# The context's key, value and output products taken out of the attention turns and put between the tiles of the q, k, v projection

## The chip, the cores and the metric

One core of one Trainium2 chip runs one program. The metric is the device time of one execution in microseconds (us), median of three runs. Engines: TensorE (PE), VectorE (DVE), ScalarE (ACT), GpSimd (POOL) and SyncE (SP), which issues every DMA here.

## The reference

A decoder layer on 16 batches of 128 tokens of width 1024, all in 32-bit floats, with a context of 16 x 128 x 1024:

```python
x = x + attn(layernorm(x))              # qkv = clip(x Wqkv^T, +-8); layer norm of q and k; 32 heads with ALiBi; Wout
x = x + xattn(layernorm(x), ctx, ctx)   # linear attention, below
x = x + ffn(layernorm(x))               # silu(x W1) * (x W3), then W2; weights unpacked from 4 bits

# xattn, per batch; q, k, v are [128, 1024] (128 tokens are the channels, 1024 the length n)
kh = softmax(Wk @ ctx, axis=-1)                    # 512 x 1024
vh = Wv @ ctx
qh = softmax(Wq @ xn, over the 64 of a head) * 64**-0.5
context = kh vh^T per head (8 heads of 64 x 64)
out = Wo @ (context^T qh) + bo ; normalised over the 128 channels, times g
```

What depends on the context alone (kh, vh, their product, and Wo on it: a matrix z of 128 x 512 for each batch) needs nothing of x.

## The kernel before

The program has three phases, one after the other. Each has a written-out instruction order for each engine, with semaphores between them.

**Projection** (`qkv_phase`, L155). x is normalised and transposed once (`LayerNormT`, L41), and split in a high and a low part of type fp32r. The weights come in 6 chunks of 512 columns, each in 8 slices of 128 x 512: SP loads a slice to one of two places in `stage` (L197), ACT writes its high part (L231), DVE the low part (L255). For each chunk, 16 tiles of 128 tokens are computed: `product` (L309) runs 24 matmuls of 512 columns (8 slices of the inner dimension by the three terms high*high, high*low, low*high). DVE clips the tile (L282), SP stores it (L217). A slice is loaded every second tile, before the wait for that tile's clip (L215, L216); ACT splits it in every even tile (L246), DVE in the odd ones (L278), so that the last slice of a chunk is split a tile before it is needed. Four PSUM banks take the tiles in turn.

**Attention** (`attention_phase`, L316). Turn b computes the self-attention of batch b ("own") and, interleaved, the cross attention of batch b-1 ("cross"); turn 0 is own alone, turn 16 cross alone. A turn has 12 steps and a tail. In step t PE does, in this order (L510): transposes of the probabilities of head group t-2 (L519), scores of group t (L527), the cross query product of tile t-2 (L537), the value product of group t-3 (L548), then the context's part: the keys of its tile (L558, t = 0, 2, 4, 6), the transposes of their exponentials (L564, t = 1, 3, 5, 7), the key by context product (L575, t = 3, 5, 8, 9), then the transposes of the query softmax (L584). In the last two steps come the value product (L589) and the output product (L595). These context products are plain 32-bit matmuls; a plain one is recorded as two matmuls. The steps' other engines: DVE sums the query's exponentials (L736), adds the bias (L481), takes the maximum (L487), the query's maximum and difference (L749, L752) and a reciprocal (L765); ACT the exponentials (L656, L662) and copies (L652, L666); POOL two scalings (L697, L708). The tail of the turn on PE: output of the cross attention (L604), first half of the Wout projection, transposes of the next q and k (L421), the norm (L626), second half of the projection, transposes of the next context (L438), and the broadcast of the norm (L643). After it DVE scales (L821) and starts the next turn's first scores.

**Feed-forward** (`feed_forward_phase`, L915): not touched.

## Time and profile before

| | |
|---|---|
| three runs | 3303.15, 3303.19, 3303.97 us; median 3303.19 |
| span of the profiled execution, first to last instruction | 3299.9 us (the page gives no other time of it) |
| busy: PE, PE weight load | 3128.8, 2393.9 us |
| busy: DVE, ACT, POOL | 1773.3, 1045.8, 507.1 us |
| mean granted clock of TensorE | 0.977 |

The page gives busy shares of each engine over the span; a row of the trace gives the start of an instruction, its length, and what ended its engine's idle time before it. Matmuls are pipelined: the record of one overlaps the next, so the time that one takes from PE is the distance between two starts, not the length of a record.

### The profile page before, as it was taken

To read this page: it belongs to the slowest core of one execution; us is meant where nothing else is said; L and a number is where in the kernel's file an instruction comes from. 1 tells how busy PE (TensorE), PEld (TensorE's weight loads), DVE (VectorE), ACT (ScalarE), POOL (GpSimd) and SP (SyncE) were. 2 spreads that over 40 slices of the span, in tenths; PEclk is the share of its full clock that TensorE was granted. 3 is DMA by queue.
4 is the path that set the end of the run, shared out by engine and by line. 5 is a ranking of instruction groups with operands and counts; after the bars stand their busy time and mean duration, and the time that the engine had idled before them with its cause. 6 is when DMAs were issued, how large, how long until landed. Compare 5 with 4: busy or idle time off the path is not lost. (4 is left out here: it accounts for less than half of the span.)

```text
span 3299.9 us, 41826 instructions
## 1 busy us (share of the span) xinstructions
PE 3128.8 (95%) x15136; PEld 2393.9 (73%) x15136; DVE 1773.3 (54%) x2927; ACT 1045.8 (32%) x2356; POOL 507.1 (15%) x525
## 2 busy tenths in 40 slices
PE   7999997799999999999996799999999899999998
PEld 6888886566666666666663688888887788888887
DVE  5311112466666666666663655555555655555555
ACT  2100000566665566666651211111111211111111
POOL 2100000233333333333332100000000100000000
PEclk9999999899999999999996899999999999999999
DMA  4222223111111111111110432222122521231222
GB/s 144 93 73 75 73 70 116 41 39 38 43 46 51 38 38 39 50 38 51 38 33 31 129 82 55 76 65 75 54 82 76 153 64 54 81 81 54 62 74 78
DMA packets 83350, 218.73 MB, mean 66 GB/s; under 512 B 11984, under 2 KB 18256, under 8 KB 81232
## 3 DMA queue, kind: packets, MB, share of 16 engines
q1 hardware_dynamic: 83280, 217.78, 21.8%
q8 instruction: 46, 0.75, 0.1%
q14 instruction: 24, 0.20, 0.0%
HBM read 175.79 MB, written 41.94 MB: 66 GB/s over the span
## 5 line engine op out<-in xcount | busy, mean ns | idle before, releaser
L312 PE MATMUL ff_ps<-h_xT_hi,w_hi 128*128 128x512 f32 x1376 | 538.2, 391 | 13.2 <-DVE h_xT_lo L96 13.2
L312 PE MATMUL ff_ps<-h_xT_lo,w_hi 128*128 128x512 f32 x1376 | 537.1, 390 | 0.0
L312 PE MATMUL ff_ps<-h_xT_hi,w_lo 128*128 128x512 f32 x1376 | 537.0, 390 | 0.0
L1042 ACT ACTIVATE w_hi<-words 128x1024 fp32r<-128x1024 f32 x134 | 142.5, 1063 | 697.3 <-DVE words L1087 697.3
L1127 DVE TENSOR_TENSOR acc<-ff_po,acc 128x512 f32<-128x512 f32 x352 | 243.0, 692 | 210.6 <-PE ff_po L312 209.9
L312 PE MATMUL qkv_acc<-w_hi,xT_hi 128*128 128x512 f32 x768 | 300.9, 392 | 9.2 <-DVE w_lo L255 9.2
L312 PEld LDWEIGHTS ff_ps<-h_xT_hi,w_hi 128*128 128x128 f32 x1376 | 259.5, 189 | 68.3 <-issue 8.8
L312 PE MATMUL qkv_acc<-w_hi,xT_lo 128*128 128x512 f32 x768 | 299.4, 390 | 0.0
L312 PE MATMUL qkv_acc<-w_lo,xT_hi 128*128 128x512 f32 x768 | 299.3, 390 | 0.0
L312 PEld LDWEIGHTS ff_ps<-h_xT_hi,w_lo 128*128 128x128 f32 x1376 | 259.4, 189 | 54.1
L312 PEld LDWEIGHTS ff_ps<-h_xT_lo,w_hi 128*128 128x128 f32 x1376 | 259.6, 189 | 53.8
L312 PE MATMUL ff_po<-w_hi,h_hi 128*128 128x512 f32 x704 | 276.3, 393 | 10.1 <-DVE h_lo L1119 10.1
L282 DVE TENSOR_SCALAR qkv_out<-qkv_acc 128x512 f32<-128x512 f32 x96 | 66.4, 692 | 395.1 <-PE qkv_acc L312 395.1
L312 PE MATMUL ff_po<-w_lo,h_hi 128*128 128x512 f32 x704 | 275.8, 392 | 0.0
L312 PE MATMUL ff_po<-w_hi,h_lo 128*128 128x512 f32 x704 | 275.6, 391 | 0.0
L1115 DVE TENSOR_TENSOR gate<-gate,ff_ps 128x512 f32<-128x512 f32 (+1 forms) x88 | 60.3, 686 | 345.4 <-PE ff_ps L312 344.7
L656 ACT ACTIVATE scores<-scores,neg_max 128x128 f32<-128x128 f32 x512 | 199.2, 390 | 120.0 <-DVE neg_max L487 120.0
L231 ACT ACTIVATE w_hi<-w_stage 128x512 fp32r<-128x512 f32 x56 | 35.4, 632 | 452.8 <-DMA w_stage<-in_w_attn 452.8
L697 POOL TENSOR_TENSOR scores<-scores,row_rec 128x512 f32<-128x512 f32 x128 | 133.2, 1041 | 293.3 <-DVE row_rec L765 293.3
L312 PEld LDWEIGHTS qkv_acc<-w_hi,xT_hi 128*128 128x128 f32 x768 | 144.6, 188 | 39.1 <-DVE w_lo L255 9.6
L1087 DVE TENSOR_TENSOR words<-words,sc 128x1024 f32<-128x1024 int32 x134 | 164.2, 1226 | 4.6
L312 PEld LDWEIGHTS qkv_acc<-w_hi,xT_lo 128*128 128x128 f32 x768 | 144.4, 188 | 30.2
(156 smaller groups left out, 5305.9 us busy)
## 6 DMA issues: line engine op xcount, KB each, us to landing
words<-in_w SPq DMA_DIRECT2D x90, 512.0 KB, 3.5
qkv<-qkv_out SPq DMA_DIRECT2D x96, 256.0 KB, 2.0
words<-in_w SPq DMA_DIRECT2D x176, 128.0 KB, 4.0
sc<-in_s SPq DMA_DIRECT2D x88, 256.0 KB, 4.3
qk_in<-qkv SPq DMA_DIRECT2D x16, 1024.0 KB, 4.9
w_stage<-in_w_attn SPq DMA_DIRECT2D x56, 256.0 KB, 3.0
qkv_rows<-in_x SPq DMA_DIRECT2D x16, 512.0 KB, 3.8
ctx_in<-in_context SPq DMA_DIRECT2D x16, 512.0 KB, 3.7
```

The lines of the kernel that those rows point to most:

```text
L231: nc.scalar.activation(dst[:, r, :], stage[:, r % 2, :], ACT.Copy).then_inc(w_hi_done, 1)
L282: nc.vector.tensor_scalar(res[:, :], acc[:, t % BANKS, :], CLIP, -CLIP, ALU.min, ALU.max).then_inc(clipped, 1)
L312: last = nc.tensor.matmul(out, left, right, start=n == 0, stop=n == len(pairs) - 1)
L656: last = nc.scalar.activation(sc[:, t % SR, j, :], sc[:, t % SR, j, :], ACT.Exp, bias=neg_max[:, t, j:j + 1], accum_out=row_sum[:, t, j:j ...
L697: nc.gpsimd.tensor_tensor(sc[:, n % SR, :, :], sc[:, n % SR, :, :], row_rec[:, n, :].unsqueeze(2).to_broadcast([P, HG, P]), ALU.mult).then ...
L1042: nc.scalar.activation(dst, src, ACT.Copy).then_inc(s["split_hi"], 1)
L1087: nc.vector.tensor_tensor(dst, src, scale, ALU.mult).then_inc(s["scaled"], 1)
L1115: nc.vector.tensor_tensor(gate[sl][0:units, :], gate[sl][0:units, :], b, ALU.mult).then_inc(s["product"], 1)
L1127: nc.vector.tensor_tensor(cols, po[:, o % 4, :], cols, ALU.add).then_inc(s["added"], 1)
```

## The change

The context's part leaves the turns and goes into the first phase, now `projection_phase`. There the tokens are taken in two halves of 8 tiles, each with all 6 chunks: 12 rounds of 8 tiles, and every weight slice is loaded and split twice. The order is written out for all 96 tiles, without loops. In rounds 1 to 4 and 7 to 10 the tiles carry the context: batch b takes four tiles, i = 0 to 3. PE does in tile (b, i): the keys of quarter i (`keys`: 2 halves by 3 terms, fp32r), 12 of the tile's 24 matmuls, in tile i = 0 the key by context product of batch b-1 (`key_context`: 24 fp32r matmuls of 512 columns), the 8 transposes of the keys' exponentials (`turn_keys`), the other 12 matmuls; after it, in i = 1 the transposes of the context, in i = 2 the value product and in i = 3 the output product of batch b-1 (both plain 32-bit). z of each batch is stored to memory (`zc`) and loaded by the attention turns. One weight slice of the next round is loaded, split high and split low in every tile. The layer norm of the second half of the tokens is made in round 5. `acc` has two PSUM banks instead of four, `res` two places instead of one. The first round's weights are loaded as four transfers of two slices to places of their own, and the first tile waits for them slice by slice. In attention, the loads of q, k and v of the next batch wait for less (`a_done`, `o_done`), `y` and `y_sq` have their own tiles, and PE's order is otherwise as before.

The core of the diff:

```diff
+    TILES = NB // 2
+    ROUNDS = 2 * QKV_CHUNKS
+    CTX_ROUNDS = (1, 2, 3, 4, 7, 8, 9, 10)
...
+    acc = pb("qkv_acc", [P, 2, N], ph)
+    room_k = pb("room_k", [P, D], ph)
+    room_t = pb("room_t", [P, D], ph)
+    room_u = pb("room_u", [P, D], ph)
...
+    def step(ci, t):
+
+        if ci in CTX_ROUNDS:
+            at = CTX_ROUNDS.index(ci) * TILES + t
+            return at // XT, at % XT
+        if ci == ROUNDS - 1 and t < XT:
+            return NB, t
+        return None, None
...
+            def load(ci, r):
+                sp.wait_ge(s["w_lo_done"], ci * KT + r - 1)
+                chunk = ci % QKV_CHUNKS if ci < ROUNDS else QKV_CHUNKS
+                sp.dma_start(stage[:, r % 2, :], w_attn[chunk, :, r, :]).then_inc(w_in[r % 2], 16)
...
+            for ci in range(ROUNDS):
+                for t in range(TILES):
+                    at = ci * TILES + t
+                    b, i = step(ci, t)
+                    load(ci + 1, t)
+                    if ci == 0 and t + 3 < TILES:
                         load_rows(t + 3)
-                    if t % 2 == 0:
-                        load(c + 1, t // 2)
-                    sp.wait_ge(clipped, c * NB + t + 1 + BANKS)
-                    sp.dma_start(qkv[t, :, bass.ds(c * N, N)], res[:, :]).then_inc(stored, 16)
-
-            chunks(sp, chunk)
-            sp.wait_ge(stored, 16 * (QKV_CHUNKS * NB + 1))
+                    if ci == 4 and t < 2:
+                        load_rows(TILES + t)
+                    if i == 3 and b + 2 < NB:
+                        load_context(b + 2)
+                    if i == 0 and b >= 2:
+                        store_z(b - 2)
+                    sp.wait_ge(s["clipped"], at + 1)
+                    sp.dma_start(qkv[ci // QKV_CHUNKS * TILES + t, :, ci % QKV_CHUNKS * N:(ci % QKV_CHUNKS + 1) * N],
+                                 res[:, at % 2, :]).then_inc(stored[at % 2], 16)
+                    if ci == 5 and t + 2 < TILES:
+                        load_rows(TILES + t + 2)
...
+            def exponential(b, i):
+                n = b * XT + i
+                act.wait_ge(s["k_maxed"], n + 1)
+                if n:
+                    act.wait_ge(s["kt_done"], n)
+                if b >= 2:
+                    act.wait_ge(s["k_recced"], 2 * (b - 1))
+                nc.scalar.activation(kE[:, :], room_k[:, :], ACT.Exp, bias=kneg[:, i:i + 1],
+                                     accum_out=ksum[:, b % 2, i:i + 1]).then_inc(s["k_exped"], 1)
+
+            def turned(b, i):
+                act.wait_ge(s["kt_done"], b * XT + i + 1)
+                nc.scalar.activation(kT_hi[:, :, i * P:(i + 1) * P], room_t[:, :].rearrange("p (a b) -> p a b", a=KT),
+                                     ACT.Copy).then_inc(s["kt_out"], 1)
...
+            for ci in range(ROUNDS):
+                if ci:
+                    act.wait_ge(s["mm_done"], ci * TILES)
+                for t in range(TILES):
+                    b, i = step(ci, t)
+                    if ci == 0 and t == TILES - 1:
+                        act.wait_ge(s["setup_in"], 3 * 16)
+                        nc.scalar.activation(wk_hi[:, :], mT[:, :], ACT.Copy).then_inc(s["wk_hi_done"], 1)
+                        split_high(0)
+                    if i == 2 and b < NB:
+                        context(b)
+                    if ci == 0 and t + 1 < TILES:
                         ln.high(act, t + 1, t + 1, turn[(t + 1) % 2])
-                    if t % 2 == 0:
-                        high(c + 1, t // 2, w_hi[1 - parity])
-
-            chunks(act, chunk)
+                    high(ci + 1, t, w_hi[1 - ci % 2])
+                    if b is not None and b < NB:
+                        exponential(b, i)
+                        if i == 3 and b + 1 < NB:
+                            split_high(b + 1)
+                        turned(b, i)
+                    if ci == 5:
+                        ln.high(act, TILES + t, t, turn[t % 2])
...
+            for ci in range(ROUNDS):
+                for t in range(TILES):
+                    at = ci * TILES + t
+                    b, i = step(ci, t)
+                    if ci:
+                        was, quarter = step(*before(ci, t))
+                        if quarter == 3 and was:
+                            z_out(was - 1)
+                    if b is not None:
+                        if b < NB:
+                            key_maxima(b, i)
+                        if i == 2 and b < NB:
+                            context_low(b)
+                        if i == 3 and b:
+                            blocks_out(b - 1)
+                        if i == 2 and b:
+                            sums(b - 1)
+                    if ci == 0 and t + 2 < TILES:
                         statistics(t + 2)
-                    if first and t + 1 < NB:
+                    if ci == 0 and t + 1 < TILES:
                         ln.low(dve, t + 1, t + 1, turn[(t + 1) % 2])
-                    if t % 2 == 1:
-                        low(c + 1, t // 2, w_hi[1 - parity], w_lo[1 - parity])
-                    dve.wait_ge(mm_done, c * NB + t + 1)
-                    dve.wait_ge(stored, (c * NB + t + 1) * 16)
-                    nc.vector.tensor_scalar(res[:, :], acc[:, t % BANKS, :], CLIP, -CLIP, ALU.min,
-                                            ALU.max).then_inc(clipped, 1)
-
-            chunks(dve, chunk)
+                    if ci == 5:
+                        if t == 0:
+                            statistics(TILES)
+                        if t + 1 < TILES:
+                            statistics(TILES + t + 1)
+                    low(ci + 1, t, w_hi[1 - ci % 2], w_lo[1 - ci % 2])
+                    if ci == 0 and t == TILES - 1:
+                        dve.wait_ge(s["wk_hi_done"], 1)
+                        nc.vector.tensor_tensor(wk_lo[:, :], mT[:, :], wk_hi[:, :].bitcast(F32),
+                                                ALU.subtract).then_inc(s["wk_lo_done"], 1)
+                        split_low(0)
+                    if i == 3 and b + 1 < NB:
+                        split_low(b + 1)
+                    if i == 0 and b:
+                        product_out(b - 1)
+                    if b is not None and b < NB:
+                        turned_low(b, i)
+                    dve.wait_ge(s["mm_done"], at + 1)
+                    if at >= 2:
+                        dve.wait_ge(stored[at % 2], at // 2 * 16)
+                    nc.vector.tensor_scalar(res[:, at % 2, :], acc[:, at % 2, :], CLIP, -CLIP, ALU.min,
+                                            ALU.max).then_inc(s["clipped"], 1)
+                    if ci == 5:
+                        ln.low(dve, TILES + t, t, turn[t % 2])
...
+            def keys(b, i):
+                n = b * XT + i
+                if i == 0:
+                    pe.wait_ge(s["split_lo"], b + 1)
+                if n:
+                    pe.wait_ge(s["k_exped"], n)
+                of, at = slice(i * P, (i + 1) * P), [slice(e * N, (e + 1) * N) for e in range(2)]
+                for e in range(2):
+                    last = product(nc, room_k[:, at[e]], [(w[:, of], c[:, at[e]]) for w, c in (
+                        (wk_hi, ctx_hi), (wk_hi, ctx_lo), (wk_lo, ctx_hi))])
+                last.then_inc(s["k_done"], 1)
+
+            def turn_keys(b, i):
+                n = b * XT + i
+                pe.wait_ge(s["k_exped"], n + 1)
+                if n:
+                    pe.wait_ge(s["kt_lo"], n)
+                for k in range(KT):
+                    last = nc.tensor.transpose(room_t[:, k * P:(k + 1) * P], kE[:, k * P:(k + 1) * P], ident[:, :])
+                last.then_inc(s["kt_done"], 1)
...
+            def key_context(b):
+                pe.wait_ge(s["kt_lo"], (b + 1) * XT)
+                pe.wait_ge(s["c_lo"], b + 1)
+                if b:
+                    pe.wait_ge(s["z_ready"], b)
+                product(nc, room_u[:, 0:N], [(c[:, k, :], e[:, k, :]) for k in range(KT) for c, e in (
+                    (ctxT_hi, kT_hi), (ctxT_hi, kT_lo), (ctxT_lo, kT_hi))]).then_inc(s["m_done"], 1)
...
+                    if ci == 1 and t == 0:
+                        pe.wait_ge(s["wk_lo_done"], 1)
+                    if b is not None and b < NB:
+                        keys(b, i)
+                    if at >= 2:
+                        pe.wait_ge(s["clipped"], at - 1)
+                    part(ci, t, range(KT // 2))
+                    if i == 0 and b:
+                        key_context(b - 1)
+                    if b is not None and b < NB:
+                        turn_keys(b, i)
+                    part(ci, t, range(KT // 2, KT)).then_inc(s["mm_done"], 1)
+                    if i == 1 and b < NB:
+                        turn_context(b)
+                    if i == 2 and b:
+                        values(b - 1)
+                    if i == 3 and b:
+                        outputs(b - 1)
+                    if ci == 5:
+                        if t == 0:
+                            pe.wait_ge(s["z_ready"], 7)
+                        if t == 1:
+                            pe.wait_ge(s["kt_lo"], 8 * XT)
+                        ln.transpose(pe, TILES + t, t % 2, turn[t % 2])
```

In `attention_phase` the branches of the steps and of the tail that name `k_tile`, `kt_tile`, `m_tile`, `transpose_context`, `context_out`, b_done, z_done and krec are deleted, and one load is added:

```diff
         if ahead:
-            sp.wait_ge(s["k_done"], (b + 1) * XT)
-            sp.dma_start(ctx_in[:, :], ctx_kv[b + 1, :, :]).then_inc(s["ctx_loaded"], 16)
-            sp.wait_ge(s["b_done"], b + 1)
+            sp.wait_ge(s["a_done"], 2 * b + 2)
...
+        if own and cross:
+            sp.dma_start(z[:, :, :], zc[b, :, :].rearrange("p (a d) -> p a d", a=XT)).then_inc(s["z_loaded"], 16)
```

## Rows read from the trace of the kernel before

**Rows 1.** Busy time of each engine by stage: stretch, its length, busy us (instructions), clock.

```profile
24.00:561.00 537.00, 536.63 (x2416) 445.04 (x2416) 139.65 (x230) 44.95 (x63) 24.59 (x28) 1.00 0.25 83
...
705.00:1726.00 1021.00, 978.83 (x5548) 647.10 (x5547) 680.13 (x1375) 635.49 (x1708) 381.44 (x392) 0.99 0.13 43
```

**Rows 2.** Groups of instructions in one turn, 1097 to 1169.6: count | busy us, mean ns | idle before.

```profile
L708 POOL TENSOR_TENSOR qr<-qr,q_rec 128x512 f32<-128x512 f32 x8 | 8.3, 1043 | 6.4 <-DVE q_rec L743 6.4
...
L558 PE MATMUL pair_k<-ctx_in,wqk_sb 128*128 128x512 f32 x16 | 7.8, 612 | 0.0
...
L564 PE MATMUL pair_k<-ident,kE 128*128 128x128 f32 x32 | 4.4, 280 | 2.2 <-ACT kE L673 2.1
L575 PE MATMUL bank_s<-kT,qk_in 128*128 128x128 f32 x32 | 4.1, 281 | 0.0
...
L575 PE MATMUL pair_o<-kT,qk_in 128*128 128x128 f32 x32 | 3.9, 275 | 0.0
...
L595 PE MATMUL pair_k<-wo_sb,cT 128*128 128x128 f32 x8 | 1.2, 288 | 0.4 <-DVE cT L770 0.4
...
L589 PE MATMUL pair_k<-qk_in,wv_sb 128*128 128x128 f32 x8 | 1.1, 275 | 0.0
```

**Rows 3.** What PE waited for in that turn: us, times, longest.

```profile
PE pair_k L564 <- ACT kE L673: 2.1, 1, 2.1
```

**Rows 4.** That turn in three stretches: first eight steps, last steps, tail.

```profile
1097.00:1128.70 31.70, 29.55 (x174) 17.38 (x173) 25.04 (x48) 26.18 (x81) 15.12 (x15) 1.00 0.22 66
1128.70:1142.30 13.60, 12.74 (x112) 10.12 (x111) 9.15 (x18) 9.00 (x20) 4.64 (x5) 1.00 0.08 16
1142.30:1166.50 24.20, 24.20 (x111) 17.14 (x110) 11.76 (x30) 10.21 (x21) 4.91 (x5) 1.00 0.08 34
```

**Rows 5.** PE at a border of two projection tiles: start us, length, instruction.

```profile
440.63 0.39 PE L312 MATMUL qkv_acc<-w_hi,xT_lo 128*128 128x512 f32 x1
440.86 0.39 PE L312 MATMUL qkv_acc<-w_hi,xT_hi 128*128 128x512 f32 x1
```

**Rows 6.** The other engines at this border: clip, store, next load, split.

```profile
441.15 0.69 DVE L282 TENSOR_SCALAR qkv_out<-qkv_acc 128x512 f32<-128x512 f32 x1 [4.15 <-PE qkv_acc L312]
...
442.02 0.33 SPq L217 DMA_DIRECT2D qkv<-qkv_out  x1
...
442.59 0.35 SPq L197 DMA_DIRECT2D w_stage<-in_w_attn  x1
...
445.79 0.63 ACT L231 ACTIVATE w_hi<-w_stage 128x512 fp32r<-128x512 f32 x1 [10.44 <-DMA w_stage<-in_w_attn]
```

**Rows 7.** A turn's key maximum, exponential, and the transposes that wait for it.

```profile
1098.58 1.09 ACT L673 ACTIVATE kE<-pair_k,kneg 128x1024 f32<-128x1024 f32 x1
...
1099.82 1.09 PE L564 MATMUL pair_k<-ident,kE 128*128 128x128 f32 x8 [2.11 <-ACT kE L673]
...
1104.98 1.23 DVE L758 TENSOR_REDUCE kneg<-pair_k 128x1 f32<-128x1024 f32 x1
```

**Rows 8.** PE's first matmul of the projection.

```profile
24.07 0.80 PE L312 MATMUL qkv_acc<-w_hi,xT_hi 128*128 128x512 f32 x1 [9.20 <-DVE w_lo L255]
```

**Rows 9.** ACT and DVE in one step of that turn.

```profile
1102.97 0.69 DVE L487 TENSOR_REDUCE neg_max<-scores 128x4 f32<-128x512 f32 x1
...
1103.69 0.40 ACT L656 ACTIVATE scores<-scores,neg_max 128x128 f32<-128x128 f32 x1 [0.30 <-DVE neg_max L487]
...
1105.24 0.61 ACT L662 ACTIVATE qr<-qr 128x512 f32<-128x512 f32 x1
...
1106.21 0.66 DVE L736 TENSOR_REDUCE q_sum<-qr 128x8 f32<-128x512 f32 x1
...
1107.50 0.69 DVE L487 TENSOR_REDUCE neg_max<-scores 128x4 f32<-128x512 f32 x1
```

**Rows 10.** Two turns, the granted clock behind POOL's busy time.

```profile
1142.30:1214.60 72.30, 69.29 (x399) 45.88 (x398) 48.49 (x99) 45.38 (x122) 27.24 (x28) 1.00 0.13 42
1214.60:1288.50 73.90, 70.89 (x399) 46.74 (x398) 48.65 (x99) 45.38 (x122) 27.24 (x28) 0.98 0.14 43
```

More of the change, by code:

```diff
@@ L193, in _ @@
         def _(sp):
-            def load(c, r, wait=True):
-                if wait:
-                    sp.wait_ge(w_lo_done, c * PIECES + r - 1)
-                sp.dma_start(stage[:, r % 2, :], w_attn[c, :, r, :]).then_inc(w_in[r % 2], 16)
-            def load_rows(t):
-                sp.wait_ge(ln.transposed, t + 1)
-                sp.dma_start(rows[:, t % 2, :], x[t, :, :]).then_inc(x_in[t % 2], 16)
-            sp.sem_inc(ln.transposed, 2)
-            for t in range(2):
-                load_rows(t)
@@ L222, in _ @@
+            store_z(NB - 1)
+            sp.wait_ge(s["z_stored"], 16 * NB)
+            for p in range(2):
+                sp.wait_ge(stored[p], 16 * ROUNDS * TILES // 2)
         @block.gpsimd
         def _(pool):
-            for t in range(NB):
-                ln.normalise(pool, t, t % 2, rows[:, t % 2, :])
+            nc.gpsimd.memset(cT[:, :, :], 0.0).then_inc(s["filled"], 1)
+            for n in range(NB):
+                ln.normalise(pool, n, n % 2, rows[:, n % 2, :])
         @block.scalar
@@ L228, in _, with high @@
         def _(act):
-            def high(c, r, dst):
-                act.wait_ge(w_in[r % 2], (c * (PIECES // 2) + r // 2 + 1) * 16)
-                nc.scalar.activation(dst[:, r, :], stage[:, r % 2, :], ACT.Copy).then_inc(w_hi_done, 1)
-            act.sem_inc(stored, 16)
-            for r in range(PIECES // 2):
+            def high(ci, r, dst):
+                if ci:
+                    act.wait_ge(w_in[r % 2], ((ci - 1) * (KT // 2) + r // 2 + 1) * 16)
+                    src = stage[:, r % 2, :]
+                else:
+                    act.wait_ge(w_first[r // 2], 16)
+                    src = first_stage(r)
+                nc.scalar.activation(dst[:, r, :], src, ACT.Copy).then_inc(s["w_hi_done"], 1)
@@ new lines, in context, with split_high @@
+            def context(b):
+                act.wait_ge(s["c_done"], b + 1)
+                nc.scalar.activation(flat(ctxT_hi[:, :, :]), room_u[:, :], ACT.Copy).then_inc(s["c_out"], 1)
+            def split_high(b):
+                act.wait_ge(ctx_loaded[b % 2], (b // 2 + 1) * 16)
+                if b:
+                    act.wait_ge(s["k_done"], b * XT)
+                nc.scalar.activation(ctx_hi[:, :], ctx_in[:, b % 2, :], ACT.Copy).then_inc(s["split_hi"], 1)
+            for r in range(KT // 2):
@@ new lines, in turn_keys, with turn_context @@
+            def turn_keys(b, i):
[6 more added lines that the diff above has]
+                last.then_inc(s["kt_done"], 1)
+            def turn_context(b):
+                if b:
+                    pe.wait_ge(s["m_out"], b)
+                for k in range(KT):
+                    last = nc.tensor.transpose(room_u[:, k * P:(k + 1) * P], ctx_in[:, b % 2, k * P:(k + 1) * P],
+                                               ident[:, :])
+                last.then_inc(s["c_done"], 1)
@@ new lines, in outputs, with part @@
+            def outputs(b):
+                pe.wait_ge(s["b_out"], b + 1)
+                for j in range(XT):
+                    last = nc.tensor.matmul(room_u[:, j * P:(j + 1) * P], cT[:, j, :], wo_sb[:, j, :], start=True,
+                                            stop=True)
+                last.then_inc(s["z_done"], 1)
+            def part(ci, t, ks):
+                hi, lo, at = w_hi[ci % 2], w_lo[ci % 2], ci * TILES + t
+                for k in ks:
+                    if ci == 0 and t == 0:
+                        pe.wait_ge(s["w_lo_done"], k + 1)
+                    for n, (a, w) in enumerate(((xT_hi, hi), (xT_hi, lo), (xT_lo, hi))):
+                        last = nc.tensor.matmul(acc[:, at % 2, :], a[:, t, k, :], w[:, k, :],
+                                                start=k == 0 and n == 0, stop=k == KT - 1 and n == 2)
+                return last
@@ L688, in turn_scalar @@
             norm_qk_affine(act, b + 1)
-            context_out(act, b + 1)
     def turn_gpsimd(pool, b, own, cross, ahead):
```

376 lines of the change are left out of this document (177 added, 199 removed).

## The prediction

> **What bounds the kernel now.** I read the stages first [rows 1]. In the projection PE is busy 536.6 of 537.0 us, DVE 139.7 and ACT 45.0: PE alone sets its time, and nothing put on PE there is hidden. In the attention turns PE is busy 979 of 1021 us, but DVE (680) and ACT (635) are far from idle. So the change moves PE work from a stage where PE is nearly full to one where it is quite full. It can gain only by what PE's products become cheaper by, by waits that go, and by what the turns give back; that last sum depends on who is the next bound in a turn.
>
> Next, one turn of 72.4 us. Its context groups on PE [rows 2] are keys 7.8, transposes 4.4, key by context 4.1 + 3.9, values 1.1 and outputs 1.2 us; the record of a group runs on 0.17 us past the start of the next (a projection matmul is 0.39 long and the next starts 0.23 later [rows 5]), and with the context's own transposes (8, like each of the four sets: 4.4 / 4 - 0.17 = 0.93) that is 21.1 us of PE's time. The only large wait of PE is 2.1 us for the first key exponential [rows 3]. The stretches [rows 4] show where PE binds: in the first eight steps PE is busy 29.6 of 31.7 us, ACT 26.2 and DVE 25.0; in the last steps 12.7 of 13.6; the tail of 24.2 us is all PE, with DVE at 11.8.
>
> **PE's work in the projection.** 96 tiles and 15 sets of transposes fill the 537 us of that stage [rows 1]: (537 - 15 x 0.93) / 96 = 5.45 us a tile, 0.227 us for each of its 24 fp32r matmuls, as between the two starts of [rows 5]. Per batch the projection gets: keys 24 x 0.227 = 5.4 (7.1 before: three cheap terms are cheaper than one plain product), transposes of the exponentials 3.7, of the context 0.9, key by context 24 x 0.227 = 5.4 (7.4 before), values and outputs 2.0. Sum 17.4 us, 16 times: **+278 us**, uncovered.
>
> **A queue on ACT in these tiles.** The new order puts `high(ci + 1, t)`, which waits for a DMA, ahead of `exponential(b, i)` on ACT, and PE's `turn_keys` in the middle of the same tile waits for that exponential. When does the slice come? Let X be the start of a tile on PE (440.86). The clip of the tile before starts at X + 0.29, its store at X + 1.16, the load of the slice at X + 1.73, and ACT starts the split at X + 4.93 and needs 0.63 [rows 6]. The new SP order is the same (load, wait for this tile's clip, store, next load), only now in every tile. From the exponential's start to PE's transposes are 1.24 us [rows 7], so PE can transpose at X + 5.5 + 1.24 = X + 6.75. PE itself is there at X + 1.36 (keys) + 2.72 (12 matmuls) = X + 4.1, in i = 2 and 3 0.9 later (context transposes, values). It waits 2.7, 1.8 and 1.8 us; in i = 0 the 24 matmuls of `key_context` (5.4) and the outputs cover it. Per batch 6.2 us, with 2.7 more for the first tile of batch 0: **+102 us**. Were the order on ACT no matter, what remains is keys' end, maximum 1.23 and exponential 1.24 with their signals, ready about 0.4 us late in three tiles of four: +20 us. DVE's other new work (low parts, copies, maxima: about 20 us of a batch's 45) lies beside PE; each piece ends before the clip, the narrowest by 0.4 us.
>
> [...]
>
> **Rounds without context.** Slice, high, low, clip, store and next load now form one chain in every tile: 3.2 + 0.63 + 0.69 + 0.69 + 0.75 = 6.0 us against 5.44 of PE. Round 6 and the end of round 11 lose some 0.5 a tile; at the borders of rounds the last slice is late by about 1 us, after round 0 by 3 (key weights and first context are split then too); in round 5 row loads, statistics, split and clip make a chain of 7.7 against 6.4. Together +15 us (0 to 30). The start: PE begins at 24.07 us [rows 8], behind a chain of eight small loads; four larger loads and waits per slice should let it begin near 17: -7 (0 to -12). The 12 rounds' doubled splits add 0.63 us ACT and 0.69 us DVE per tile, both covered outside the chains named.
>
> **What a turn gives back.** PE would need only 72.4 - 21.1 - 2.1 = 49 us, but look at a step without the context [rows 9]: a maximum ends (1103.66), ACT's four exponentials run 1103.69 to 1105.24, the query's exponential 0.61 more, DVE then sums it (the sum starts 0.03 later), and from that start to the end of the next maximum are 1108.19 - 1106.21 = 1.98. This ring takes 0.03 + 1.55 + 0.61 + 0.03 + 1.98 = 4.2 us with no PE in it. The five intervals from the third maximum to the end of the first stretch of [rows 4] take 25.0 us, 5.0 each. They give back 4.0 us; the first two steps nothing. The last steps: after the last maximum, exponentials 2.2, then twice sum, reciprocal, maximum, difference and exponential (2.9 each), then sum, reciprocal, POOL's 1.04 [rows 2], transposes and copy (3.2): 11.3 to 11.5 against 13.6, so 2.1. The tail stays PE's, less its context transposes, of which DVE lets through 0.5. A turn gets 6.6 shorter. I take off 1.0 for the clock: one of two neighbouring turns has a granted clock of 0.98 and is 1.6 us longer, the other 1.00 [rows 10] (0.99 over the stage [rows 1]), and with values and outputs gone PE pauses more at the end of the steps, just ahead of the tail. So 5.5 x 15 turns = 83; turn 0, with no query work, some 11: **-94 us**. Bounds: 0, and 23 x 16 = -370 if PE's remaining work were the bound.
>
> **Sum**: 278 + 102 + 15 - 7 - 94 = +294 on the profiled 3299.9; the median stands 3.3 above that span, so 3597 us. The feed-forward phase is untouched. No change means within 0.2% (6.6 us), about what a measurement of this kernel can tell.
>
> **The rivals.** (1) *The slice is there in time or does not hold up the exponential*: the waits shrink to 20 and the tile chains to 5: 3303 + 278 + 20 + 5 - 7 - 94 = 3505 us. For it: a slice takes 2.6 us at best, and small shifts add up over tiles; against it: the order on SP ties the load to the clip of the tile before, as in [rows 6]. (2) *The clock falls in the new tiles*: PE pauses 2.7 us and then only transposes, in 48 tiles. At half clock the second half of a tile takes 2.7 us more, and a moment of it cost a turn 1.6 [rows 10]: 48 x 1.6 = 77, so 3674 us. Against it: the turn of [rows 4] has the pause of [rows 3] and a clock of 1.00 in all three stretches. The Trainium skill ("TensorE: Matmul & The Clock Gate", section on HAM oscillation) warns of loops in which bursts of matmuls are parted by waits, and pay for the slower clock again and again; by that rule the estimate is (2). (3) *Faster*: the turn falls to PE's 49 us, and ACT's queue does not matter: 3505 + 94 - 370 = 3229 us. It decides at a turn shorter by more than (278 + 18) / 16 = 18.5 us without the waits; with them not even 23 a turn suffice (3303 + 388 - 370 = 3321). For it: PE is the busiest engine of [rows 4]. Against it: the ring of [rows 9] holds no PE, and the tail of 24.2 is there anyway; only 16 of the 31.7 us could be left of the steps. (4) *The change does less than it says*, the context still waiting in the turns for z: z of a batch is stored hundreds of us before, so hardly.
>
> **Chances.** Forecast 0.60 (its own range 3545 to 3655); (1) 0.15; (2) 0.13; (3) 0.06; nothing measurable 0.02; the rest between and beyond. The range 3475 to 3665 takes in (1) and half of (2) and leaves out under 2 in 10. Faster 0.06, same 0.02, slower 0.92.
>
> **What would show it.** First PE matmul near 17 us; projection ending near 950 instead of 561; in a batch's second to fourth tile a PE wait of about 2 to 3 us before `turn_keys`, ended by ACT's exponential, which itself starts right behind a weight split that waited for its DMA, tiles 10.4 us apart; the first tile of a batch without a wait. Turns of about 67 us with PE idle in the steps, maxima 4.2 us apart, tails of 24. The forecast is wrong if turns take 60 us or less, or if these tiles are under 9 us apart.

## The result, and the profile of the changed kernel

The changed kernel takes 3610.93 us (median of 4 runs, 3607.76 to 3614.04) against 3303.17 before (3301.11 to 3303.97): a ratio of 1.0931, 95% interval 1.0917 to 1.0944. It is slower by 308 us, as forecast in sign and nearly in size (3597). The profiled span is 3606.0 us, 306.1 more than before.

The page of the changed kernel, lines 1 and the clock of part 2:

```profile
span 3606.0 us, 40415 instructions
PE 3189.0 (88%) x14624; PEld 2389.1 (66%) x14624; DVE 1914.4 (53%) x2976; ACT 1087.5 (30%) x2421; POOL 508.7 (14%) x525
PEclk9999999999799999999999979999999999999999
```

PE has 512 matmuls fewer and is busy 60 us longer, yet the span grew by 306, so its idle time grew by 246 us. Where, the stages say (as in [rows 1]; the columns are length, busy us of PE, PEld, DVE, ACT, POOL, then clock, DMA share, GB/s):

```profile
15.10:936.00 920.90, 831.19 (x4082) 685.50 (x4080) 404.81 (x536) 243.21 (x336) 27.21 (x28) 0.99 0.25 76
...
1061.00:2032.00 971.00, 783.41 (x3641) 436.45 (x3641) 574.17 (x1149) 499.18 (x1526) 380.36 (x392) 0.92 0.11 40
...
2113.00:3606.00 1493.00, 1445.50 (x6368) 1196.46 (x6368) 832.66 (x1074) 262.51 (x327) 30.00 (x32) 0.98 0.27 78
```

The projection ends at 936 instead of 561, with PE idle for 90 us in it where it had been idle for 0.4. In 14 turns PE is now busy 783 of 971 us (979 of 1021 before), at a clock of 0.92, where it had been 0.99. The feed-forward phase is what it was (some 1499 us in both).

What PE waited for in the projection (us in total, times, longest), and over the whole run in the turns:

```profile
PE room_t L492 <- ACT kE L304: 81.6, 49, 2.8
PE qkv_acc L533 <- DVE w_lo L354: 2.7, 1, 2.7
```

```profile
PE bank_q L770 <- DVE qr L934: 93.5, 102, 1.7
...
PE bank_p L752 <- POOL scores L879: 56.4, 26, 4.4
```

49 waits before `turn_keys`: three in each of 16 batches, and one for the first tile. This is the queue of the prediction. One of these tiles (b = 3, i = 3) in the timelines of SP, DVE, ACT and PE (start, length):

```profile
279.80 0.33 SPq L271 DMA_DIRECT2D qkv<-qkv_out  x1
280.18 0.43 SPq L225 DMA_DIRECT2D w_stage<-in_w_attn  x1
```

```profile
281.35 1.23 DVE L363 TENSOR_REDUCE kneg<-room_k 128x1 f32<-128x1024 f32 x1 [1.58 <-PE room_k L577]
...
284.03 0.63 ACT L295 ACTIVATE w_hi<-w_stage 128x512 fp32r<-128x512 f32 x1 [6.67 <-DMA w_stage<-in_w_attn]
284.56 1.10 ACT L304 ACTIVATE kE<-room_k,kneg 128x1024 f32<-128x1024 f32 x1
```

```profile
283.64 0.39 PE L533 MATMUL qkv_acc<-w_hi,xT_lo 128*128 128x512 f32 x1
285.80 1.09 PE L492 MATMUL room_t<-ident,kE 128*128 128x128 f32 x8 [1.77 <-ACT kE L304]
```

Read it from below: PE has done its 12 matmuls and waits 1.77 us for the exponential (L304). The exponential starts as the split (L295) ends, and in front of the split ACT had been idle 6.67 us for the DMA, which SP issued 0.38 us after the store of the tile before. DVE's maximum had ended at 281.35 + 1.23 = 282.58, so the exponential (start 284.56) stood ready for 2 us behind an instruction that it does not need.

In the turns PE's product for y, the cross attention's output, begins like this; the second row is of the run `e5_fill_end` below, in which the same 8 records are at full clock:

```profile
1337.41 6.69 PE L800 MATMUL bank_s<-qT,z 128*128 128x512 f32 x8 [0.86 <-ACT qT L857]
```

```profile
1396.46 3.69 PE L810 MATMUL bank_s<-qT,z 128*128 128x512 f32 x8 [0.16 <-ACT qT L867]
```

6.69 us for what takes 3.69 otherwise: most of what my sum had wrong in the turns. From the first of these records to the first of the product's second half there are 4.9 to 6.6 us in the 15 turns that have both halves of the work (mean 5.7); before there were 3.44 in every one.

### The profile page after: what moved, and what is told of

Its sections match the earlier page's. It is cut to its first block and busy times, and to the rows that moved or that the text cites. A ratio compares the mean times of both kernels' runs of the same rounds, so it can differ in the third digit from the quotient of the medians.

```text
span 3606.0 us, 40415 instructions
## 1 busy us (share of the span) xinstructions
PE 3189.0 (88%) x14624; PEld 2389.1 (66%) x14624; DVE 1914.4 (53%) x2976; ACT 1087.5 (30%) x2421; POOL 508.7 (14%) x525
## 5 line engine op out<-in xcount | busy, mean ns | idle before, releaser
L533 PE MATMUL qkv_acc<-w_hi,xT_hi 128*128 128x512 f32 x768 | 310.5, 404 | 2.7 <-DVE w_lo L354 2.7
L770 PE MATMUL bank_q<-wq_sb,xn 128*128 128x512 f32 x256 | 157.6, 700 | 95.5 <-DVE qr L934 93.5
L295 ACT ACTIVATE w_hi<-w_stage 128x512 fp32r<-128x512 f32 x98 | 61.7, 631 | 499.0 <-DMA w_stage<-in_w_attn 499.0
L76 POOL TENSOR_TENSOR ln_moments<-ln_moments,half_neg 128x1 f32<-128x1 f32 x32 | 21.3, 666 | 1194.3 <-DVE ln_moments L69 1177.2
L760 PE MATMUL bank_s<-kD,qkT 128*128 128x512 f32 x256 | 152.6, 681 | 28.8 <-DVE scores L712 22.2
```

Source lines behind the costliest of these rows:

```text
L76: nc.gpsimd.tensor_tensor(self.moments[:, p, 4:5], self.moments[:, p, 3:4], self.half_neg[:, :], ALU.pow).then_inc(self.rstd_done, 1)
L295: nc.scalar.activation(dst[:, r, :], src, ACT.Copy).then_inc(s["w_hi_done"], 1)
L533: last = nc.tensor.matmul(acc[:, at % 2, :], a[:, t, k, :], w[:, k, :], start=k == 0 and n == 0, stop=k == KT - 1 and n == 2)
L760: nc.tensor.matmul(bank_s[:, :], qkT[:, 0, t, :], flat(kD[:, t, :, :]), start=True, stop=True).then_inc(s["s_done"], 1)
L770: nc.tensor.matmul(bank_q[:, :], xn[:, n * P:(n + 1) * P], wq_sb[:, :], start=True, stop=True).then_inc(s["q_done"], 1)
```

## The experiments

Each edit is against the changed kernel unless it says otherwise. Distances between clips (`qkv_out<-qkv_acc` on DVE) and between maxima (`neg_max<-scores`) are differences of starts in the timeline; a turn is measured from one first record of y to the next.

**1. ACT's order turned round.**

```diff
-                    high(ci + 1, t, w_hi[1 - ci % 2])
                     if b is not None and b < NB:
                         exponential(b, i)
+                    high(ci + 1, t, w_hi[1 - ci % 2])
+                    if b is not None and b < NB:
                         if i == 3 and b + 1 < NB:
                             split_high(b + 1)
                         turned(b, i)
```

> The changed kernel with one order on ACT turned round: in a context tile the exponential of the keys comes first, then the split of the weight slice that waits for its DMA. Nothing else is touched. In the profile of the changed kernel PE waits 81.6 us in all before the transposes of the exponentials (49 times, longest 2.8). Theory (ACT's queue: the exponential stands behind a split that waits for a DMA): these waits fall to about 20 us in all (what is left of maximum and exponential), the second to fourth tiles of a batch come 9.2 to 9.6 us apart instead of 9.9 and 10.6, and the kernel takes about 3550 us (3611 - 61). Rival A (PE waits for the chain maximum, exponential itself, and the DMA is in time anyway): 3605 to 3613 us, waits as before. Rival B (the wait is only handed on: the split now comes later, with it low part, clip and next load, and PE waits for the accumulator instead): 3585 to 3615 us, with new PE waits ended by DVE's clip.

Measured: 3515.15 us (ratio to the kernel before 1.0639, 1.0621 to 1.0657), 96 us less than the changed kernel, more than the 61 expected. The wait before `turn_keys` is gone from the list of PE's waits, not reduced to 20. ACT and PE in one tile:

```profile
235.02 1.12 ACT L304 ACTIVATE kE<-room_k,kneg 128x1024 f32<-128x1024 f32 x1 [4.33 <-DVE kneg L364]
...
237.19 0.63 ACT L295 ACTIVATE w_hi<-w_stage 128x512 fp32r<-128x512 f32 x1 [0.97 <-DMA w_stage<-in_w_attn]
```

```profile
236.28 1.09 PE L493 MATMUL room_t<-ident,kE 128*128 128x128 f32 x8
```

The split still waits for its DMA, now behind the exponential, and PE's row has no idle time in its brackets. The tiles i = 1, 2, 3 are 7.8, 8.7 and about 8.9 us apart; in the changed kernel they were some 9.9, 10.0 and 10.6. These are PE's own sums (24 matmuls 5.44, keys 1.36, transposes 0.93: 7.73, and 0.93 more for context or value work), so my expected 9.2 to 9.6 was too high as well. The clips of the projection now span 818.7 us. Rivals A and B fall: one exchange of two instructions on an engine that is 30% busy was worth 96 us.

**2. The slices loaded one tile earlier, ACT's order untouched.**

```diff
+            load(1, 0)
             for ci in range(ROUNDS):
                 for t in range(TILES):
...
-                    load(ci + 1, t)
+                    if at + 1 < ROUNDS * TILES:
+                        load(ci + 1 + (t + 1) // TILES, (t + 1) % TILES)
```

> The changed kernel with every load of a weight slice issued one tile earlier on SP (the slice of tile t + 1 before the wait for the clip of tile t); ACT's order stays, split first. Theory (the DMA is what holds the split and so the exponential): the slice is there when ACT comes to it, the PE waits before the transposes fall from 81.6 to about 20 us, and the chains of the tiles and round borders without context lose their DMA too: 3611 - 61 - 10 = about 3540 us, a little below the kernel with the exponential first. Rival A (ACT is late for another reason: copies, the chain of maximum and exponential): 3605 to 3613 us. Rival B (what counts is the place of the split, 0.63 us long, ahead of the exponential even with its data there): half of the gain or less, 3570 to 3600 us.

Measured: 3506.39 us (1.0607, 1.0589 to 1.0625), 105 us less than the changed kernel, where about 70 were expected. ACT in a tile with the exponential still behind the split:

```profile
237.01 0.62 ACT L297 ACTIVATE w_hi<-w_stage 128x512 fp32r<-128x512 f32 x1
238.72 1.12 ACT L306 ACTIVATE kE<-room_k,kneg 128x1024 f32<-128x1024 f32 x1 [1.09 <-DVE kneg L365]
```

Now the exponential waits for the maximum and for nothing else. The same waits are gone by another way, so it is the two together, a DMA that lands late and a queue in which it stands first, and either remedy does. From the first to the last clip of the projection there are 808.5 us. In the kernel before there are 529.5 (31.2 to 560.7), so the context's work costs (808.5 - 529.5) / 16 = 17.4 us of PE a batch, the forecast's own figure, and nothing is left over for the halves of tokens. The changed kernel needs 912.6 (23.0 to 935.6).

**3. No context in the projection.**

```diff
-        if ci in CTX_ROUNDS:
-            at = CTX_ROUNDS.index(ci) * TILES + t
-            return at // XT, at % XT
-        if ci == ROUNDS - 1 and t < XT:
-            return NB, t
         return None, None
...
+            nc.gpsimd.memset(z[:, :, :], 0.01).then_inc(s["filled"], 1)
```

> The changed kernel without the whole context branch in its projection (keys, exponentials, their transposes, key by context, values, outputs are left out and z is a constant that is stored 16 times); the two halves of tokens, the doubled splits and the turns stay. Theory (the context's work and waits are all that the projection got, the halves cost some 15 us): projection from the first matmul near 15 to about 568 us, turns 69.4 us apart as in the changed kernel, 3611 - 368 = about 3243 us. So the change without its moved work would be 60 us faster than the kernel before. Rival (the halves themselves are dear: twice the slices, twice the splits, the second six rounds with row loads): projection of 590 us or more, 3265 us or more. Second rival (the context's tail effects reach into the turns): turns shorter or longer than 69.4 by over 1 us.

Measured: 3257.18 us (0.9852, 0.9836 to 0.9869), where 3243 was expected. This kernel leaves out the context's part, so its time stands for no finished layer. The projection's clips run from 21.8 to 579.7, 557.9 us, 28.4 more than before, where 15 were expected. Turns are 69.4 us apart as in the changed kernel. PE's waits in its projection:

```profile
PE qkv_acc L530 <- DVE w_lo L351: 15.4, 11, 2.6
```

Eleven borders of rounds, each with PE waiting for the last slice: the loads are tied to the clip of the tile before, the last one too. The rest of the 28 is round 5, whose tiles are 7.1 to 7.5 us apart against 6.35 for the same work in the first chunk before, and single longer tiles. The changed kernel itself shows this border wait once (2.7): elsewhere the context's work covers it. With the loads ahead (run 2) it is gone.

**4. Plain products in place of three terms.**

```diff
-                    last = product(nc, room_k[:, at[e]], [(w[:, of], c[:, at[e]]) for w, c in (
-                        (wk_hi, ctx_hi), (wk_hi, ctx_lo), (wk_lo, ctx_hi))])
+                    last = product(nc, room_k[:, at[e]], [(wk_hi[:, of].bitcast(F32), ctx_hi[:, at[e]].bitcast(F32))])
...
-                product(nc, room_u[:, 0:N], [(c[:, k, :], e[:, k, :]) for k in range(KT) for c, e in (
-                    (ctxT_hi, kT_hi), (ctxT_hi, kT_lo), (ctxT_lo, kT_hi))]).then_inc(s["m_done"], 1)
+                product(nc, room_u[:, 0:N], [(ctxT_hi[:, k, :].bitcast(F32), kT_hi[:, k, :].bitcast(F32))
+                                             for k in range(KT)]).then_inc(s["m_done"], 1)
```

> The changed kernel with plain fp32 products in place of the three-term ones for keys (2 of 512 columns a tile) and key by context (8 of 512 columns a batch); they take the high parts alone, so the low parts of keys, weights and context do not enter the result, and all splits still run. In the kernel before, a plain product of 512 columns takes 0.88 us (7.1 / 8), three cheap ones 0.68. Theory (ACT waits for the DMA in the second to fourth tile, so longer keys there hide in PE's wait): +0.4 us in the first tile's keys, +1.6 us in key by context, 2.0 x 16 = +32: about 3643 us, with the PE waits before the transposes shorter by some 20 us in all. Rival A (nothing hides, PE pays all): 4 x 0.4 + 1.6 = 3.2 a batch, +51: 3662 us. Rival B (the three-term form buys nothing here): 3605 to 3617 us.

Measured: 3633.48 us (1.0998, 1.098 to 1.1017), 23 us more than the changed kernel (32 expected, 51 if nothing hid). The first tile of a batch takes 15.89 us instead of 14.04; the three others stay at 9.9 to 10.5, and PE's wait there fell by 22 us:

```profile
PE room_t L491 <- ACT kE L304: 59.3, 48, 2.4
```

Where PE ran into the wait anyway, the longer product cost nothing: part of what the three-term form saves was thrown away in the queue on ACT.

**5. Unread matmuls in PE's pauses of the turns.**

```diff
+    FILL = {2: 10, 9: 5, 10: 5, 11: 5}
+    def fill(n):
+        for k in range(n):
+            nc.tensor.matmul(bank_n[:, :], w_hi[0][:, k % KT, 0:P], w_hi[1][:, k % KT, :], start=True, stop=True)
...
         for t in range(STEPS):
+            if cross and own:
+                fill(FILL.get(t, 0))
...
         if cross:
+            if own:
+                fill(3)
             pe.wait_ge(s["d_out"], (c + 1) * KT)
```

> The changed kernel with matmuls that nobody reads, put where PE pauses in turns 1 to 15: 10 before the transposes of step 2, 5 before each of steps 9, 10 and 11, 3 before the product for y (28 fp32r matmuls of 512 columns, 0.227 us each, 6.4 us a turn). Nothing else is touched. In the profile of the changed kernel 7 of y's first 8 records run at half clock (0.86 us apart, 0.43 later), and turns take 69.4 us where 67.4 were forecast (66.8 in the mean over PE's tail). Theory (PE's pauses at the end of the steps and before step 2 cost the clock, and the clock costs the missing time): the work of the fill lies in pauses, the y product runs at full clock (2.7 us less) and step 2 too (0.5 to 1 less): turns of 66 to 67 us, 3611 - 15 x 3 = about 3566 us. Rival A (the clock falls whatever PE does there, or the pauses are not what it answers to): PE is only given more work, turns 69.4 to 71 us, 3611 to 3635. Rival B (the fill is late and delays the transposes that the copies wait for): turns over 71 us.

Measured: 3572.95 us (1.0819, 1.0802 to 1.0835), 38 us less, though PE has 28 matmuls a turn more to do. The turn falls from 69.4 us in the mean to 65.9 in most turns (mean of 14: 66.1). Three stretches of a turn, first of the changed kernel (y to the next turn's first maximum, first to last maximum, the rest), then of this run:

```profile
1337.40:1366.20 28.80, 27.43 (x102) 17.69 (x102) 12.35 (x27) 9.17 (x20) 6.48 (x9) 0.89 0.03 9
1366.20:1394.90 28.70, 22.21 (x110) 9.83 (x110) 20.73 (x42) 18.57 (x70) 15.58 (x16) 0.94 0.14 52
1394.90:1407.50 12.60, 6.87 (x50) 3.47 (x48) 8.39 (x16) 7.95 (x19) 5.12 (x5) 0.90 0.25 90
```

```profile
1396.50:1422.50 26.00, 24.61 (x103) 16.75 (x104) 12.44 (x28) 9.18 (x20) 6.74 (x9) 1.00 0.04 10
1423.00:1450.00 27.00, 22.16 (x118) 10.56 (x118) 19.69 (x41) 18.46 (x70) 14.82 (x14) 1.00 0.14 52
1450.00:1462.40 12.40, 10.24 (x69) 6.32 (x68) 8.18 (x16) 7.96 (x19) 5.22 (x5) 1.00 0.27 98
```

The clock is 1.00 in all three instead of 0.89 to 0.94. The tail is 1.4 to 3 us shorter (25.8 from y to the next maximum, against 27.2 to 28.8), the second and third distances of maxima are 3.23 and 4.24 instead of 3.9 to 4.35 and 4.24 to 4.42. In this run's profile the projection was some 6 us longer than in the changed kernel (its clips end at 941.3), with waits of PE before `turn_keys` of 87.1 us instead of 81.6. From the last clip to the end the profiled run is 47.7 us shorter (3564.0 - 941.3 against 3606.0 - 935.6). Two of the turns were 67.4 us instead of 65.9. Which of the places of the fill paid, step 2, the last steps or the one before y, was not measured one by one.

**6. The same kind of matmuls in the steps.**

```diff
+    FILL = {3: 4, 4: 4, 5: 4, 6: 4, 7: 4, 8: 4}
```

> The changed kernel with 4 unread fp32r matmuls (0.91 us) before each of steps 3 to 8 of turns 1 to 15, 5.4 us more of PE's work a turn in the steps alone. Theory (the steps are a ring of DVE, ACT and POOL of 4.24 us without PE, which is busy 21.7 of 28.6 us there): maxima stay 4.24 us apart and the turn stays at 69.4 us: 3605 to 3620 us. That would show that the first 5 us or so of what the change took off PE in a step were free to take, and gave nothing back. Rival (PE is still in the ring of a step, through the transposes and the query product): each step 0.3 to 0.9 us longer, turns of 71 to 75 us, 3640 to 3690 us. Second rival (the pauses in the steps are what lowers the clock of the tail): turns of 67 us, 3575 us.

Measured: 3617.62 us (1.0951, 1.0935 to 1.0968). Turns stay 69.4 us apart in the mean and the maxima 4.24, from the fourth on (the third distance is 4.24, 4.4 or 4.68). The 7 us more than in the changed kernel lie in the projection, whose clips end at 942.7 in the profile, 7.0 later. PE's busy time in the same stretch:

```profile
1373.40:1402.10 28.70, 25.65 (x127) 13.73 (x128) 20.30 (x41) 18.46 (x70) 15.48 (x15) 0.94 0.13 47
```

25.7 us instead of 22.2 in the same 28.7: the steps have room for this much on PE and return none of it when it is taken away. So PE does not bound them. What does is the ring, the closed chain of instructions that repeats from one maximum to the next. In the changed kernel:

```profile
1381.94 0.69 DVE L718 TENSOR_REDUCE neg_max<-scores 128x4 f32<-128x512 f32 x1
...
1382.67 0.40 ACT L847 ACTIVATE scores<-scores,neg_max 128x128 f32<-128x128 f32 x1 [1.59 <-DVE neg_max L718]
...
1384.22 0.61 ACT L853 ACTIVATE qr<-qr 128x512 f32<-128x512 f32 x1
...
1384.87 0.69 DVE L918 TENSOR_REDUCE q_sum<-qr 128x8 f32<-128x512 f32 x1 [0.34 <-ACT qr L853]
...
1386.18 0.69 DVE L718 TENSOR_REDUCE neg_max<-scores 128x4 f32<-128x512 f32 x1
```

ACT starts 0.04 us after the maximum ends, DVE's sum 0.04 us after ACT's last exponential ends, and the next maximum follows 4.24 us after the last one. It is the forecast's ring of DVE and ACT. POOL's scalings are not in it, though the expectation above counts POOL in. The last stretch of this turn, not shown, had a clock of 1.00, and the next tail is 27.9 us long, within the 27.2 to 28.8 of the changed kernel: this fill moves the low clock but does not end it.

**7. What paid, together.** Edits 1, 2 and 5.

> The changed kernel with what paid in the earlier runs put together: the exponential ahead of the split on ACT, each slice loaded one tile earlier on SP, and the unread matmuls in the pauses of turns 1 to 15 (10 before step 2, 5 before steps 9 to 11, 3 before y). Theory (three separate losses: DMA waits in the projection, chains at borders, clock in the turns): projection as with the earlier loads (first to last clip 808.5 us), turns 65.9 us, 3506 - 15 x 3.5 = 3454 us. It is then PE's added work alone that keeps the change behind: 16 x 17.4 = 278 in the projection, against 16 x 6.9 given back by turns. Rival (the losses overlap: without pauses in the projection or at another phase the clock in the turns differs): 3470 to 3510 us.

Measured: 3457.83 us (1.046, 1.0444 to 1.0476), expected 3454. The three losses add up. It is still 154 us behind the kernel before: what remains is 16 x 17.4 = 278 us of PE's work in a stage where PE is the bound, against turns that give back some 6.7 each in the mean.

**8. The kernel before, with the changed kernel's start.**

```diff
+    with ExitStack() as early:
+        first_in = sb("first_in", [P, KT, N], F32, early)
     xT_lo = sb("xT_lo", [P, NB, KT, P], F32R, ph)
...
-            for t in range(2):
-                load_rows(t)
-            for r in range(PIECES):
-                load(0, r, r >= 2)
+            load_rows(0)
+            for n in range(KT // 2):
+                if n == 1:
+                    load_rows(1)
+                sp.dma_start(first_in[:, 2 * n:2 * n + 2, :],
+                             w_attn[0, :, 2 * n:2 * n + 2, :]).then_inc(w_first[n], 16)
```

ACT and DVE split from `first_in`, and PE's first tile waits slice by slice. The place is free because `xT_lo` gets its first values only after these slices are split.

> The kernel before with one part of the change alone, its start: the first chunk's weights come as four transfers of two slices each, all issued at once, to a place of their own (where the later batches' low parts will lie), and the first tile waits slice by slice. Before, PE's first projection matmul is at 24.07 us; in the changed kernel at 15.1. Theory (the start is worth what the first matmul comes earlier, since PE alone bounds the projection from there on): 3303.2 - 7 to 9 = 3294 to 3296 us. Rival (PE then runs into the rows and their transposes in the first chunk, and the gain is lost by its end): 3300 to 3304 us.

Measured: 3290.23 us (0.9957, 0.9943 to 0.9971), 13 less than before in the medians and 11.6 between the profiled spans, more than the 7 to 9 expected. PE's first projection matmul ([rows 8] had 24.07):

```profile
14.42 0.78 PE L317 MATMUL qkv_acc<-w_hi,xT_hi 128*128 128x512 f32 x1
```

9.7 us earlier. The first clip is 10.5 us earlier (20.7 against 31.2), and from it to the last there are 529.5 us as before.

**9. That start, and a fill in the kernel before.**

```diff
+            if own and cross and t == 1:
+                pe.wait_ge(s["y_scaled"], b)
+                for k in range(8):
+                    nc.tensor.matmul(flat(bank_d[:, :, :]), w_hi[0][:, k, 0:P], w_hi[1][:, k, :], start=True, stop=True)
             if own and (i := kt_tile(t)) is not None:
                 pe.wait_ge(s["k_exped"], b * XT + i + 1)
```

> The kernel before with the early start (3290 us by itself, turns in it 72.24 us apart, every third 73.88) and 8 unread fp32r matmuls in PE's 2.1 us pause of step 1, ahead of the transposes of the first key exponential, in turns 1 to 15. Theory (the third turn's 1.64 us is the clock falling in that pause, as in the turns of the changed kernel): all turns 72.2 us, 3290 - 5 x 1.64 = 3282 us. Rival A (the slow moments there come from elsewhere): 3289 to 3292 us. Rival B (the fill is longer than the pause and delays the key exponentials' transposes, in a stage where PE binds): 3292 to 3305 us.

Measured: 3280.37 us (0.9926, 0.9912 to 0.994). One slow turn of the start kernel of experiment 8, and two turns and a bit of this one:

```profile
1056.30:1130.20 73.90, 70.89 (x399) 46.79 (x398) 48.56 (x99) 45.38 (x122) 27.25 (x28) 0.98 0.14 43
```

```profile
760.00:912.00 152.00, 148.82 (x867) 99.90 (x866) 101.01 (x206) 94.93 (x251) 56.57 (x58) 1.00 0.13 42
```

All turns are now 72.24 us, none 73.9; 3282 us were expected. Of the kernels that leave nothing out this is the fastest, 0.74% ahead of the kernel before, and it has nothing of the moved context in it.

## Why the prediction was right, and which term was off

Of the forecast's +294, by its own steps, against the 306.1 between the spans:

| step | forecast | measured |
|---|---|---|
| start | -7 | first clip 31.2 to 23.0: -8 |
| PE's work moved to the projection | +278 | 808.5 - 529.5 (run 2): +279 |
| ACT's queue, and rounds without context | +102, +15 | 912.6 - 808.5: +104 together |
| turns | -94 | last clip to PE's last matmul of attention, 1240.2 to 1170.8: -69 |

The sum came within 12 us partly by luck: the queue and the rounds without context cost 13 us less than forecast, and the turns gave back 25 us less.

**PE's work**: right to the microsecond. Counting matmuls by the 0.227 us of [rows 5] and the transposes of [rows 2] is enough where PE binds before and after.

**ACT's queue**: the mechanism is shown twice, by turning the order (run 1) and by bringing the DMA forward (run 2). The size was 81.6 us of waits where I had 102. The load goes out earlier than I had it: the store starts 0.72 us after the clip, not 0.87, and the load 0.38 us after the store, not 0.57 as in [rows 6]. Over 48 tiles that is some 16 us. Against this, the load takes longer in the tiles i = 3, where SP issues the next context 0.5 us behind it: 3.8 us from issue to split in the median, against 3.1 and 3.3 in i = 1 and 2. The forecast also said that 20 us would be left in any case, from keys, maximum and exponential: nothing is left, PE's transposes find the exponential done (run 1). Rival (1), the kernel without the queue, was put at 3505 us, and runs 1 and 2 measured 3515 and 3506; that agrees so well only because these 20 us and the 25 us that the turns failed to give back stand against each other.

**Rounds without context**: the 15 forecast were for chains in rounds 6 and 11 that did not come (5.5 us a tile), while round 5 is near where it was put (most tiles 7.2 to 7.4 us, 7.7 forecast). The term is inside the 104. The exchange on ACT took 94 of these away (912.6 to 818.7), so the queue cost up to 94 and everything else some 10.

**The clock in the new tiles**, rival (2): fell as a large term. The projection's clock is 0.99. Of the 104 us some 15 are recorded as no wait of PE, against 77 us priced. About half of that lies in four tiles that took 1 to 2.4 us more than their like (11.8 instead of 10.6, 12.0 and 12.3 instead of 9.9, 11.0 instead of 10.0). In three of the four the granted clock did fall to its lower level: it is 0.50 in stretches that begin at 104.4, 264.9 and 357.0 us, and once more at 483.3, at the border to round 6. So the rival's mechanism is real here, but it struck 3 of 48 tiles. The rest is not taken apart.

**Turns**: here the step that failed is the 1.0 us taken off for the clock. The forecast had 11 us for turn 0 and 83 for the 15 others. Turn 0 gave 14 (last clip to turn 1's first maximum, 98.1 to 84.0 us) and all later turns together 55. Means of 14 turns, in three parts as above:

| part of a turn | before | changed | with fill (run 5) | forecast of the gain |
|---|---|---|---|---|
| first to last maximum | 32.1 | 28.7 | 27.7 | 4.0 |
| last maximum to y | 14.3 | 12.6 | 12.7 | 2.1 |
| y to the next first maximum | 26.4 | 28.0 | 25.8 | 0.5 |

Steps and last steps gave 3.4 and 1.6, near the forecast, and the ring of 4.2 us was measured as 4.24. One term of it was assumed and not read: in [rows 9] the sum starts 0.36 us behind the query's exponential (1105.24 + 0.61 to 1106.21), since DVE is at the key maximum of [rows 7] until then. Without the context it is 0.04, as the forecast's 0.03 had it. The tail, which was to give 0.5, got 1.6 longer. I had read in [rows 10] that one turn of some was 1.6 us longer and took that as the measure of what the clock could do. In the kernel before PE hardly pauses between the steps and the tail. In the changed kernel it is busy 6.9 of 12.6 us there, and the y product that follows ran wholly or partly at half clock in every turn: its first half took 5.7 us in the mean instead of 3.5 with the fill, 2.2 more, and the steps lost another 1.0 (28.7 against 27.7 with the fill). With the fill a turn gives back 6.7 us in the mean (72.8 to 66.1), against 6.6 forecast before the deduction. So the right deduction was 2.2 + 1.0 = 3.2. The Trainium skill ("TensorE: Matmul & The Clock Gate", section on HAM oscillation) warns of bursts of matmuls parted by waits, which pay for the slower clock each time. I had weighed this rule against the projection's new tiles, where it hardly showed (0.99); it held in the turns (0.92), where I had allowed 1 us for it.

**Rival (3)**, turns at PE's 49 us, fell with the measured 69.4, and run 6 shows why: 3.4 us more of busy time on PE in the steps changed nothing. The turn is bound by the ring in the steps and by PE in the tail, and what is taken off PE between these two limits is lost. The fourth rival, z late, does not appear: PE's list has no wait for z in the turns.

**What stays open.** I did not try a smaller move, nor the three-term keys inside the turns of the kernel before. Whether any share of the context would pay in the projection follows only by argument: a microsecond there costs a microsecond, and turns return at most 6.9 of 23, in the runs at hand.

## What to carry to other kernels

Moving work off an engine pays only down to the next bound of the stage that it leaves, and costs its full length in a stage that this engine already bounds. So look for the ring that remains in the emptied stage before counting the gain. In an in-order queue, an instruction that waits for a DMA must not stand ahead of one that another engine is waiting for, however idle the queue's engine is: here 81.6 us of waits on PE came from the order of two instructions, and vanished when they were exchanged. And when a busy TensorE gets pauses, price the work behind the pauses at half clock too, and measure cheap filler there: it paid at the places of run 5 and not at those of run 6.

## What I had not expected of the hardware

- Giving PE 28 unread matmuls a turn (6.4 us of work) made most turns 3.5 us shorter (3.1 to 3.2 in the mean), in run 5 and again in run 7, because the granted clock stayed at its upper level (1.00, which is 2.4 GHz) instead of falling to the lower one (1.2 GHz) for a while in each turn. 8 in the kernel before removed the 1.6 us that every third turn had lost.
- It depends on where they are: 24 such matmuls in the steps alone (run 6) left the turn at 69.4 us.
- Pauses of 1.0 to 2.8 us stood in 49 places of the projection, and the clock fell in 3 of those tiles, while in the turns it fell each time. In the projection 12 or 24 matmuls at a stretch surround the pause; in the turns' last steps PE is busy 6.9 of 12.6 us in small pieces. What decides between the two no run here separates.
